# Layer norms on two engines: epsilon, power, negated mean and centre all on GpSimd

## The reference

```python
def _layernorm(x, axis=-1, eps=1e-05):
    m = jnp.mean(x, axis=axis, keepdims=True)
    v = jnp.var(x, axis=axis, keepdims=True)
    return (x - m) / jnp.sqrt(v + eps)

# layer 0, first half: retention and an MLP
h = _layernorm(x) * (1 + ca) + sa                                 # norm "in"
sig = sigmoid(h @ W_ret + b_ret); ret = running mean of sig       # xi = 0.5 s + 0.5 carry
h = layernorm(h + ret, ln1)                                       # norm "mid"
out = layernorm(h + gelu(h @ W1 + b1) @ W2 + b2, ln2)             # norm "out"
x = x + ga * out
# layer 0, second half: 16 experts
h = _layernorm(x) * (1 + cb) + sb                                 # norm "x1"
rms = jnp.sqrt(jnp.mean(xf * xf, axis=-1, keepdims=True) + EPS)   # norm "rms"
logits = (xf / rms * norm_weight) @ router_weight.T + router_bias # top-1024 tokens per expert, MLP, scatter back
# layer 1, first half: a convolution whose 31 taps come from a softmax per token and head
h = _layernorm(x) * (1 + ca) + sa                                 # norm "in"
v = conv(h) @ W_fc.T + h
v = (v - mu) / jnp.sqrt(var + 1e-6) * gamma + beta                # norm "mid"
x = x + ga * v
# layer 1, second half: an MLP
h = _layernorm(x) * (1 + cb) + sb                                 # norm "x3"
x = x + gb * (relu(h @ W1 + b1) @ W2 + b2)
```

## Time and profile before

| | |
|---|---|
| runs timed | 3679.86, 3683.22, 3690.17 us |
| span of the profiled execution, first to last instruction | 3672.0 us |
| TensorE busy | 3305.8 us (90%) |
| VectorE busy | 2605.7 us (71%) |
| ScalarE busy | 1996.3 us (54%) |
| GpSimd busy | 1273.7 us (35%) |
| TensorE's share of the chain that ended last | 80% |
| VectorE's share of that chain | 10% |
| TensorE busy between 500 and 600 us (stage one) | 99.16 us of 100 |
| TensorE busy between 2600 and 2700 us (stage three) | 96.34 us of 100 |

### The profile page before, as it was taken

The page is one execution under the profiler, slowest core; times in us unless marked ns, Lnnn a source line. Parts: engine busy times, 40 slices in busy tenths (PEclk is TensorE's granted clock), DMA queues, the critical chain, the costliest instruction groups (busy, mean ns, idle before and its releaser), DMA issues.

```text
span 3672.0 us, 66560 instructions
## 1 busy us (share of the span) xinstructions
PE 3305.8 (90%) x25034; PEld 2779.9 (76%) x25034; DVE 2605.7 (71%) x5975; ACT 1996.3 (54%) x3890; POOL 1273.7 (35%) x1081
## 2 busy tenths in 40 slices
PE   7999999999971399999999358999999999999999
PEld 4888888888861299999999336777777777777788
DVE  6777777777767744454544378888888888888864
ACT  4666666666641155555555235555555555555544
POOL 2333333332321256666665333332223323222210
PEclk9999999999995599999999679999999999999999
DMA  4333222222112144444443365555555555555541
GB/s 170 123 102 99 92 94 95 76 82 76 48 42 48 57 99 103 104 100 104 98 95 61 87 117 117 122 117 118 122 122 117 121 121 122 117 121 121 105 98 41
DMA packets 745750, 365.05 MB, mean 99 GB/s; under 512 B 551370, under 2 KB 695990, under 8 KB 745302
## 3 DMA queue, kind: packets, MB, share of 16 engines
q1 hardware_dynamic: 716758, 317.78, 35.0%
q0 software_dynamic: 28672, 43.02, 6.3%
HBM read 223.73 MB, written 136.97 MB: 98 GB/s over the span
## 4 chain that ended last, share of the span: by engine, by line
PE 80%; DVE 10%; issue 3%; ACT 3%; POOL 1%; DMA 1%; SPq 1%; POOLq 0%; ACTq 0%; DVEq 0%
PE bank L1349 10%; PE bank L1333 10%; PE bank L1951 9%; PE bank L1965 9%; PE bank L826 8%; PE bank L805 8%; PE bank L1922 7%; PE bank L122 5%; PE bank L782 3%; PE bank L1933 3%; PE bank L1902 2%; DVE hits L1142 2%; ACT xh_ L530 2%; PE bank L1897 1%; PE bank L1931 1%
## 5 line engine op out<-in xcount | busy, mean ns | idle before, releaser
L1625 POOL TENSOR_TENSOR energies<-energies,energy 128x496 f32<-128x496 f32 x128 | 162.3, 1268 | 780.3 <-DVE energies L1791 780.3
L1273 DVE TENSOR_TENSOR hidden_low<-bank,hidden_high 128x512 fp32r<-128x512 f32 x256 | 176.8, 691 | 317.8 <-ACT hidden_high L1083 281.4
L1965 PE MATMUL bank<-l_w_high,l_hidden_low 128*128 128x256 f32 x1024 | 301.9, 295 | 43.3 <-DVE l_hidden_low L1853 43.3
L697 DVE TENSOR_TENSOR gT_low<-bank,gT_high 128x512 fp32r<-128x512 f32 x256 | 173.1, 687 | 212.6 <-ACT gT_high L577 212.6
L571 ACT ACTIVATE bank<-bank,b 128x512 f32<-128x512 f32 x256 | 170.2, 665 | 272.1 <-PE bank L805 269.2
L1076 ACT ACTIVATE bank<-bank,fc_bias 128x512 f32<-128x512 f32 x256 | 170.0, 664 | 267.5 <-PE bank L1333 252.5
L826 PE MATMUL bank<-w_high,gT_low 128*128 128x256 f32 x1024 | 308.5, 301 | 2.1 <-DVE gT_low L697 2.1
L1922 PE MATMUL bank<-bandT,window 128*32 128x96 f32 x5632 | 270.5, 344 | 23.9 <-issue 20.8
L826 PE MATMUL bank<-w_high,gT_high 128*128 128x256 f32 x1024 | 289.3, 282 | 0.0
L826 PE MATMUL bank<-w_low,gT_high 128*128 128x256 f32 x1024 | 289.2, 282 | 0.0
L1965 PE MATMUL bank<-l_w_high,l_hidden_high 128*128 128x256 f32 x1024 | 288.9, 282 | 0.0
(11 more groups left out here) (300 smaller groups left out, 10586.0 us busy)
## 6 DMA issues: line engine op xcount, KB each, us to landing
bandT<-bands SPq DMA_DIRECT2D x352, 240.0 KB, 3.5
fc_full<-in_L_ffn_fc_wT SPq DMA_DIRECT2D x32, 1024.0 KB
bands<-zeros SPq DMA_DIRECT2D x22, 768.0 KB, 8.5
x<-in_L_attn_x SPq DMA_DIRECT2D x32, 512.0 KB, 6.1
moe_output<-zeros SPq DMA_DIRECT2D x32, 512.0 KB, 6.7
x_after_retention<-x SPq DMA_DIRECT2D x32, 512.0 KB, 3.0
moe_input_and_gates<-xn SPq DMA_DIRECT2D x32, 512.0 KB, 4.1
x<-x_after_retention SPq DMA_DIRECT2D x32, 512.0 KB, 5.5
```

The source lines that it names most:

```text
L697: v.tensor_tensor(t.gT.low[:, g % SLICES, :], K.banks[t.bank["expand", i, g, 0]][:, :], t.gT.high[:, g % SLICES, :], ALU.subtract).then_in ...
L1273: v.tensor_tensor(t.hidden.low[:, n % SLICES, :], K.banks[t.bank["expand", i, f, 0]][:, :], t.hidden.high[:, n % SLICES, :], ALU.subtract) ...
L1965: p = pe.matmul(K.banks[6 + ch // 2][:, left:left + D], x, w, start=False, stop=f == KF - 1 and j == 2 and ch % 2 == 1)
```

## The change

VectorE's `moments` stops at the four `bn_aggr`; the last of them now signals. The addition of epsilon and the negation of the mean are `tensor_scalar` instructions on GpSimd, in `root` and `root_and_center`, in the order epsilon, power, negated mean, centre. Between GpSimd's own dependent instructions stand waits on new semaphores (`var_root`, `less_mean`). The step `rms` on VectorE is gone: GpSimd waits for ScalarE's four sums itself. Each norm has its own `stats` tile. The four loads of layer 1's MLP count on semaphores of stage one in place of four of their own (`later`).

```diff
     "modulate_out": 43.81, "squares": 44.07, "rms": 45.06, "root_rms": 46.83, ...      # "rms" is gone
...
-    t.stats = K.tile(ctx, "stats", [P, C, 6])
+    t.stats = {n: K.tile(ctx, f"stats_{n}", [P, C, 6]) for n in kinds[:4]}
...
     def root(kind, signal, i):
-        e.wait_ge(s(signal), i + 1)
+        e.wait_ge(s(signal), i + 1 if kind != "rms" else C * (i + 1))
+        if i == 0:
+            e.wait_ge(*K.setup("vector", "minus_half"))
+        source = t.sumsq[i % 2][:, :] if kind == "rms" else t.moments[kind][:, :, 1]
+        e.tensor_scalar(t.var[kind][:, :], source, 1e-5, None, ALU.add).then_inc(s("var_root"), 1)
+        roots_so_far.up()
+        e.wait_ge(s("var_root"), roots_so_far.n)
         e.tensor_tensor(t.root[kind][:, :], t.var[kind][:, :], t.minus_half[:, :], ALU.pow).then_inc(s(f"root_{kind}"), 1)

     def root_and_center(kind, taken, i):
         if i >= 1:
             e.wait_ge(s(taken), i)
         root(kind, f"var_{kind}", i)
+        e.tensor_scalar(t.less_mean[kind][:, :], t.moments[kind][:, :, 0], -1.0, None, ALU.mult).then_inc(s("less_mean"), 1)
+        taken_so_far.up()
+        e.wait_ge(s("less_mean"), taken_so_far.n)
         e.wait_ge(s(f"root_{kind}"), i + 1)
         e.tensor_tensor(t.center[kind][:, :], t.less_mean[kind][:, :], t.root[kind][:, :], ALU.mult).then_inc(s(f"center_{kind}"), 1)
...
-def moments(v, step, c, stats, moments, var, source, n, eps, signal, less_mean=None):
+def moments(v, step, c, stats, moments, source, n, signal):
...
     for i in range(n):
-        v.bn_aggr(moments[:, i, :], stats[:, i, :]).then_inc(step, c.up())
-    v.wait_ge(step, c.n)
-    if less_mean is not None:
-        v.tensor_scalar(less_mean, moments[:, 0:n, 0], -1.0, None, ALU.mult)
-    v.tensor_scalar(var, moments[:, 0:n, 1], eps, None, ALU.add).then_inc(signal, 1)
+        m = v.bn_aggr(moments[:, i, :], stats[:, i, :])
+    m.then_inc(signal, 1)
...
-        elif name == "rms":
-            v.wait_ge(s("sumsq"), C * (i + 1))
-            v.tensor_scalar(t.var["rms"][:, :], t.sumsq[i % 2][:, :], 1e-5, None, ALU.add).then_inc(s("var_rms"), 1)
...
# stage three has the same edits; in its center_mid:
-            v.bn_aggr(mean, t.stats[:, k, :]).then_inc(step, c.up())
-            v.wait_ge(step, c.n)
+            v.bn_aggr(mean, t.stats["mid"][:, k, :]).then_inc(s("l1_var_mid"), 1)
+            v.wait_ge(s("l1_var_mid"), HC * n + k + 1)
...
-            if k == HC - 1:
-                v.tensor_scalar(t.var["mid"][:, :], t.moments["mid"][:, :, 1], 1e-6, None, ALU.add).then_inc(s("l1_var_mid"), 1)
```

More of the change, by code:

```diff
@@ L157, in setup, with later @@
         return self.sem(f"{engine}_setup"), SETUP[engine].index(event) + 1
+    def later(self, name, value=0):
+        earlier, before = EARLIER[name]
+        return self.sem(earlier), before + value
     def dram(self, name, shape):
@@ L499, in retention_pool @@
         elif name == "root_rms":
-            root("rms", "var_rms", i)
+            root("rms", "sumsq", i)
         elif name == "affine_mid":
@@ L689, in retention_vector @@
                 v.wait_ge(s("center_mid"), i)
-            moments(v, step, c, t.stats, t.moments["mid"], t.var["mid"][:, :], lambda n: mid_chunk(K, t, i, n), C, 1e-5, s("var_mid"),
-                    t.less_mean["mid"][:, :])
+            moments(v, step, c, t.stats["mid"], t.moments["mid"], lambda n: mid_chunk(K, t, i, n), C, s("var_mid"))
         elif name == "expand":
@@ L700, in retention_vector @@
             v.wait_ge(s("v_part"), K.KF * (i + 1))
-            moments(v, step, c, t.stats, t.moments["out"], t.var["out"][:, :], out_chunk, C, 1e-5, s("var_out"))
+            moments(v, step, c, t.stats["out"], t.moments["out"], out_chunk, C, s("var_out"))
         elif name == "center_out":
             v.wait_ge(s(f"rows_in{i // t.PER % 2}"), 16 * (i // t.PER // 2 + 1))
+            v.wait_ge(s("var_out"), i + 1)
             if i >= 2:
@@ L1442, in layer_one_tiles @@
     t.out_full = t.o[:, 0:2, :]
-    t.stats = K.tile(ctx, "l1_stats", [P, HC, 6])
+    t.stats = {n: K.tile(ctx, f"l1_stats_{n}", [P, HC, 6]) for n in ("in", "mid", "x3")}
     kinds = ("in", "mid", "x3")
@@ L1580, in layer_one_pool @@
     e.wait_ge(*K.setup("pool", "exponents"))
+    taken_so_far, roots_so_far = Count(), Count()
     def root(kind, n):
-        e.wait_ge(s(f"l1_var_{kind}"), n + 1)
+        e.wait_ge(s(f"l1_var_{kind}"), (n + 1) * (HC if kind == "mid" else 1))
+        e.tensor_scalar(t.var[kind][:, :], t.moments[kind][:, :, 1], 1e-6 if kind == "mid" else 1e-5, None, ALU.add).then_inc(s("l1_var_root"), 1)
+        roots_so_far.up()
+        e.wait_ge(s("l1_var_root"), roots_so_far.n)
         e.tensor_tensor(t.root[kind][:, :], t.var[kind][:, :], t.minus_half[:, :], ALU.pow).then_inc(s(f"l1_root_{kind}"), 1)
@@ L1589, in root_and_center @@
         root(kind, n)
+        e.tensor_scalar(t.less_mean[kind][:, :], t.moments[kind][:, :, 0], -1.0, None, ALU.mult).then_inc(s("l1_less_mean"), 1)
+        taken_so_far.up()
+        e.wait_ge(s("l1_less_mean"), taken_so_far.n)
         e.wait_ge(s(f"l1_root_{kind}"), n + 1)
@@ L1666, in layer_one_scalar @@
             (n,) = args
-            e.wait_ge(s(f"l1_mlp{n}"), 16)
+            e.wait_ge(*K.later(f"l1_mlp{n}", 16))
             e.copy(quarters[n][0].high, mlp_full(t, n, quarters[n][2])).then_inc(s("scalar_setup"), 1)
```

20 lines of the change are left out of this document (10 added, 10 removed).

## The result

The changed kernel takes 3716.57 us (median of 4 runs, 3712.76 to 3721.84) against 3681.54 us (4 runs, 3677.49 to 3690.17): 35.0 us more, ratio 1.0096 with a 95% interval of 1.0082 to 1.0111. It is slower. The forecast was 3692 us, and the range ended at 3716.

A forecast was written before the change was run, and what follows sets the result against it. TensorE bounds the kernel, waiting for `xh_` in stage one and `l_hidden_low` in stage three. 4.6 + 2.8 + 1.5 = +8.9 us on the 3672.0 span gives 3681; keeping the median's 11.2 us distance, 3692 us, range 3681 to 3716.

The forecast's parts named there:

- The place of the bound: TensorE waits for `xh_` in stage one (29 periods, 0.3 us each) and `l_hidden_low` in stage three (43.3 us).
- Part 1: Norm "mid" of stage one: chain from last `bn_aggr` to centre grows 0.16 us a tile, +4.6 us over 29.
- Part 2: Norm "in" of stage one, behind GpSimd's root of "x1": centre ends 0.5 us late, costing nothing, thinly covered.
- The spare up to the cast: In stage one, `gT_low` on VectorE still finds ScalarE's cast after L571 ready, with about 0.08 us to spare.
- the slower rival: GpSimd's `tensor_scalar` is dearer (0.35 us) and norm "in" of stage one goes late too: 3716 us, chance 0.31.
- The sign named for part 2: In stage one, `gT_low` before the statistics of "mid" coming later would show part 2 wrong.
- Part 3: VectorE's relief in stage one: seven small instructions a tile go, but L741 takes over the wait for GpSimd; zero gain.
- Part 4: Stage three: removing `l_var_mid` from VectorE gains nothing, since L1834 needs GpSimd's root; +0.2 us a batch, +2.8 us.
- Part 5: Edges: some nine norm chains without other work at stage one's start, stage three's ends and last "rms": +1.5 us.
- The median: Whole kernel: the timed median lies 11.2 us above the profiled span of 3672.0; this distance was kept in the forecast.
- The dearer rival: Same as the slower rival: GpSimd's `tensor_scalar` at 0.35 us, 3716 us; chance 0.31.
- The lock: VectorE and GpSimd share a port pair in SBUF; who holds it keeps it for the whole instruction.

The follow-up runs named there:

- the three kernels above: The changed kernel (3716.57 us); the changed kernel with the negated mean ahead of the power (3702.55 us); the changed kernel with VectorE keeping the negated mean (3694.30 us).
- the control: The changed kernel's form (own statistics tiles, semaphores, later waits), but VectorE makes epsilon and negated mean in every norm as before: 3677.90 us, ratio 0.9993.
- The kernel with 2.5 us as its longest: The kernel before, with VectorE taking the first low half of the hidden rows ahead of the MoE addition and the next slice's masked energies: 3689.88 us.
- The kernel whose waits were short: The kernel before, with VectorE taking both low halves of the hidden rows early in stage three: 3666.04 us, ratio 0.9963.
- the three others with the same order: Both low halves early on the changed kernel (3696.70 us), on the kernel without epsilon and negation (3658.74 us), and with every norm kept on VectorE (3662.85 us).

## Why the prediction was wrong, step by step

- **The place of the bound was right.** `xh_` in stage one, `l_hidden_low` in stage three. With no slack at the first, each lengthening counted 29 times, and with "mid" alone the waits for `xh_` and the time grew by the same 12.3 us.
- **Part 1 was mis-sized.** +4.6 us forecast; the kernel with "mid" alone measured +12.3. Norm "mid" is 0.41 us longer, not 0.16. Of the missing 0.25, the two `tensor_scalar` account for 0.08 (0.31 and 0.33 from start to start, where 0.20 and a wait made 0.28), the hand-over for 0.02, and 0.15 lie behind the power: the negated mean starts 1.12 us behind the power's start (512.87 to 513.99), not 0.97. I had let neighbours overlap there by 0.04, as two powers do, and the trace shows a gap of 0.08 instead.
- **Part 2 is the step that failed**: "Cost nothing, but thinly covered", decisive from a price of 0.28. At 0.23 it cost +15.5 us. The failed term is the sum that gives the start of `center_in`: 2.78 us behind that of epsilon of "x1", and it was 3.09: 0.31, 1.01, 0.33, 1.12 and 0.32, each 0.03 to 0.15 over my figure. The cover itself was read well. VectorE's instruction starts 3.00 us behind that epsilon (503.23 to 506.23; I had 3.01), so there were 0.23 us of room up to the port, and five small errors of one sign, 0.31 together, used them up and 0.09 more. The spare up to the cast was read well too: by my figures `xh` could start 0.09 us behind VectorE's instruction, by the three kernels above some 0.12. With `xh` 0.56 us later than reckoned, half of it from the sum and the rest from the port, `gT_low` and the statistics of "mid" were 0.44 late. With norms "x1" and "in" alone the sum did it without the port. From there the chain was as the slower rival described it: ScalarE, then `gT_low`, then the statistics of "mid". The sign named for part 2, `gT_low` later, is what came.
- **Part 3 was right.** L753 begins 1.16 us ahead of the end of GpSimd's product and is held to it, where it had begun with that end; two kernels without the instructions have a period of 32.02, the control 32.03.
- **Part 4 was right in mechanism and sign**, +2.8 forecast and +5.4 measured (interval 2.6 to 9.2). Epsilon ended with the stretched L1819, as said. The size was too small: forecast were 0.2 us a batch; the two waits for `l_hidden_low` of a batch without half clock are 3.35 + 0.51 us for 2.79 + 0.79, 0.28 more, and such a batch is 94.10 us for 93.60, of which 0.22 is not traced. The granted clock was missing too: the profile of after has 51.7 us at 0.50 against 23.4. The medians do not part the two.
- **Part 5**, +1.5: what is left of 35.0 after the three terms is 1.8 to 3.3, within what these medians can tell.
- **The median** was kept 11.2 us above the profiled span. Of that distance 1.8 us lie outside the span, the rest was one execution's luck: before's median is 9.5 us above its profiled span, after's 0.2 us below its own. The prediction's sum, set against the median, was right to keep it; it says nothing of the change.

Of the 26 us between +8.9 and +35.0, part 2 is 15.5, part 1 is 7.7 and part 4 is 2.6. The first two are for the most part one error, links on GpSimd reckoned 0.03 to 0.15 us too short. The dearer rival had the chance 0.31, and its time of 3716 was met within 1 us by a smaller price than it asked. In part that is luck: it had stage one at 28 us and stage three at 2.8, where 26.3 and 5.4 were measured.

The lock that the prediction took from the Trainium skill, SBUF — State Buffer, section SBUF: two separate sides, fits the pairs shown: of two that met, the one that began second was held (0.44 for 0.20, 3.80 for 1.67, 1.20 for 0.68, 1.89 for 1.19). At 0.03 us apart it did not show: `center_in` took its 0.20 there.

The Trainium skill, Perfetto Trace Analysis, section GPSIMD Engine Instruction, adds that GpSimd's instructions are to be timed "by the start-to-start spacing of consecutive instructions", not by the reported duration. This trace agrees: the row says 1.04 for both `root_x` and `root_mid`, but the instruction behind starts 1.01 us after the one and 1.12 after the other.

What stays open: why the negated mean follows a power 0.11 us later than an epsilon does, though it waits for nothing of it; why a wait of 2.8 us is followed by half clock in one batch and not in the next; why the kernel without epsilon and negation ran most of its executions at a lower clock. An edit in which GpSimd's product waits until VectorE has done the residual was thought of and not tried.

## What to carry to other kernels

Where a step is called covered, add up every link of the chain by start-to-start spacings and ask what a tenth of a microsecond in the sum does: here 0.23 us of cover stood against five links that were each 0.03 to 0.15 us longer than reckoned. A small instruction on GpSimd costs its spacing, and it can meet the port on top: look at which two-input VectorE instruction starts within 0.1 us of it, and before moving any GpSimd or VectorE instruction earlier ask what it will stand beside. And of a stall that ends last, look at the one behind it in the same batch, and move both.

## What the hardware showed that was not expected

- GpSimd's `tensor_scalar` on 128x4 takes 0.23 to 0.24 us against 0.20 for a two-input multiplication of the same size, and 0.31 to 0.33 from start to start with a dependent power.
- Beside VectorE's two-input instruction a 0.20 us instruction of GpSimd took 0.44, and VectorE's of 1.67 took 3.80 beside a 2.46 us product of GpSimd: they had begun 0.09 and 0.13 us behind the other. Begun 0.03 behind, `center_in` took 0.20.
- The granted clock fell to 0.50 behind waits of 2.5 to 3.8 us and not behind waits of 1.3. A wait of TensorE so costs more than its own length: batches of before are 93.60 us without such a stretch and some 94.15 with one of 3.4 us; batches of after 94.10 without and some 95.6 with one of 6.8 us. The longest wait alone does not tell: the kernel with 2.5 us as its longest had 40.2 us at 0.50, before with 2.9 had 23.4.
- The scatter of before, 7 to 21 us by group, went with this clock (in the group of 11 runs 0.953 at the lowest time, 0.942 at the highest). The kernel whose waits were short had 3.2 us where before had 20.7 beside it; the three others with the same order had 1.4, 3.3 and 8.8, and 8.8 is no less than before's 7.0 in that group.
